# Five half tiles of the projection move from early slots to the last two

## The chip, the cores and the metric

The kernel runs on one core of one Trainium2 chip. Its engines are TensorE (PE; its weight loads are PEld), VectorE (DVE), ScalarE (ACT), GpSimd (POOL) and SyncE (SP, which issues the DMAs). Each engine works through its own instructions strictly in the written order and waits on semaphores for the others. The metric is the device time of one execution in microseconds, as a median of several runs; lower is better.

## The reference, cut to what matters

The input has 4 batches of 256 channels by 1024 tokens. It is normalised over the channels and over groups, turned into q, k and v by a convolution of 16 taps, and put through an attention of 4 heads; then a convolution of 5 taps projects the result, the residual is added, and a table step works on the normalised tokens.

```
qkv = conv1d_same(group_norm(xf, gn_gamma, gn_beta), qkv_w, qkv_b)
h = qkv_attention(qkv)
h = conv1d_same(h, proj_w, proj_b)
return (xf + h).reshape(b, c, *spatial)
...
x = x + _L0_conv_ref(_ln_c(x), ...)
t = _to_tokens(x)
t = t + _L0_ffn_ref(_ln_t(t))
```

The change touches the order in which the second convolution, the projection, is worked on beside the last piece of attention.

## The kernel before, in words

**Steps and slots.** Two pairs of heads times 4 batches make 8 steps of convolution. The attention of a step runs one step later, beside the next convolution. In the last step (the one that the change touches) there is no convolution left: the last attention runs beside the projection of the first three batches, and the projection of batch 3, which needs the result of that attention, follows. Each engine's program walks through slots 0 to 25. Slots 0 to 15 hold the 16 attention units, slots 16 and 17 the rest of the attention, slots 18 to 25 one projection tile of batch 3 each.

**An attention unit** is a score product on PE (L1372, into the PSUM tile psS or psT in turn), a maximum on DVE (L1713), a scaled copy and an exponential on ACT (L1104, L1111), a reciprocal on DVE (L1736), a scaled copy on ACT (L1121, the high half of the probabilities) and the low half on DVE (`prob_low`, L1690, issued one slot later). A DMA turns the result over, and PE multiplies it with the values (`second_product`, L1349 and L1353, one for two units, in the odd slots; the last two products, 6 and 7, both stand at the end of slot 17). Every second product but one completes a quarter of the heads, which is copied out by ACT (L951), summed on DVE (`heads_sum`, L1697), split by ACT (L960) and by DVE (`heads_low`, L1705). `second_product` 6 waits for the `heads_sum` of the quarter before it, because both use the PSUM tile psV.

**The projection** has 32 tiles, 8 for each batch. A tile is two halves of 15 matmuls (L1190): one half for each pair of heads; the second reads `staging`. Tile q is summed in one of three PSUM banks, cM, cP and cQ, in turn (`bank[q % 3]`). DVE then adds both parts to the residual (L1581, L1583) and takes statistics of the tile before (L1569); the second of these instructions gives the bank free. So the first half of tile q waits until DVE has emptied tile q - 3:

```
else:
    pe.wait_ge(S["pj_used"], q - 2)
```

After 8 tiles come the statistics, the norm (L254 to L1627, with a square root on ACT, L840) and the table step (L1643 to L1680) of that batch, in slots of their own. POOL adds the residual and the bias for each batch (`base`, L711 and L713, two long instructions) after ACT has scaled it (L931).

**The order.** In each slot DVE first takes its part of the attention (maximum, `prob_low` of the unit before, sums of heads, reciprocal), and after that the projection tiles whose second half lies in this slot on PE. PE takes the score product, then the halves of the slot, then the second product. A table, `halves`, says how many halves a slot holds; `beside` makes the slot of each half of the first three batches of it:

```
beside = [i for i in range(SLOTS) for _ in range(halves[i])]
for b in range(NB):
    for i in range(8):
        for p in range(PAIRS):
            late(beside[16 * b + 2 * i + p] if b < 3 else SLOTS + i, "tile", b, i, p)
```

The lists of ACT, POOL and SP for the last step do not depend on this table.

Of the kernel before, what the change touches and what calls it, by code (L numbers as in the profile page):

```python
# [42 lines left out]
UNITS = 16  # L43
SLOTS = 18
# [13 lines left out]
def build(nc, x_tok, w_qkv, b_qkv, gamma, beta, w_proj, b_proj, ident_in, group_in, ramp_in, out_tok):  # L58
    with ExitStack() as ctx:
# [261 lines left out]
                late(slot, "base", b, 2 * q)  # L321


        halves = [2 if i in (0, 4, 8, 12, 15, 16) else 3 for i in range(SLOTS)]
        assert sum(halves) == 3 * 16
        beside = [i for i in range(SLOTS) for _ in range(halves[i])]
        for b in range(NB):
# [1588 lines left out]
```

## Time and profile before

| what | value |
|---|---|
| median of 3 runs | 1009.72 us (1006.71 to 1011.4) |
| the profiled execution's own time | 1011.98 us |
| its span, first to last instruction | 1010.2 us |
| PE busy | 922.1 us (91%) |
| DVE busy | 736.9 us (73%) |
| ACT busy | 664.5 us (66%) |
| POOL busy | 348.2 us (34%) |
| mean granted TensorE clock | 0.978 |
| last step, first score product of its attention | 841.88 us |
| first projection matmul of batch 3 | 967.71 us |

The busy share is a mean over the whole kernel. The last step takes the last 168 us, and there PE, DVE, ACT and POOL wait for one another in turn; what a moved instruction is worth has to be read in that stretch, wait by wait. A matmul's duration in the rows overlaps with the next one's, so the time from start to start is the one to count with: 15 matmuls of a half begin 1.64 us after the 15 before them.

### The profile page before, as it was taken

The page shows a single profiled execution, that of the slowest core. Times are in us where ns is not written, and L with a number is a line of the kernel's source. Part 1 is how long each engine was busy: PE and PEld are TensorE (multiplying, and loading weights), DVE is VectorE, ACT ScalarE, POOL GpSimd, SP SyncE. Part 2 cuts the span into 40 slices and gives each one's busy share as a digit, 9 for nine tenths or more (in the row PEclk, how much of TensorE's full clock was granted, in tenths as well). Part 3 has the DMA queues.
Part 4 walks back from the last instruction along what each step waited for, and adds up shares of the span by engine and source line. Part 5 has one row for each costly group of instructions (what it writes and reads, how often), then busy time and mean ns, then how long its engine had stood idle before and what let it go on. Part 6 is the DMA issues. An engine that isn't in the chain of part 4 may idle for free.

```text
span 1010.2 us, 19614 instructions
## 1 busy us (share of the span) xinstructions
PE 922.1 (91%) x7826; PEld 739.4 (73%) x7826; DVE 736.9 (73%) x1234; ACT 664.5 (66%) x1112; POOL 348.2 (34%) x225
## 2 busy tenths in 40 slices
PE   2587889998999999999999999999999999898784
PEld 1476678786877787877788887887887868776663
DVE  6998958774777578897785656465646776879877
ACT  5758557783778378877886767465657585576531
POOL 2687934331550245365511211021102113313410
PEclk9989799999999999999999999999999999999987
DMA  8060235978798847576637544554656863362422
GB/s 297 1 220 23 84 139 117 217 176 205 166 223 191 197 105 157 129 209 133 127 85 189 137 84 111 154 104 91 130 137 153 183 174 73 97 137 68 107 62 84
DMA packets 291866, 138.32 MB, mean 137 GB/s; under 512 B 269120, under 2 KB 271552, under 8 KB 291264
## 3 DMA queue, kind: packets, MB, share of 16 engines
q1 hardware_dynamic: 291776, 137.08, 55.6%
q8 instruction: 62, 1.02, 0.4%
q14 instruction: 28, 0.23, 0.1%
HBM read 48.80 MB, written 16.95 MB: 65 GB/s over the span
## 4 chain that ended last, share of the span: by engine, by line
PE 56%; DVE 17%; ACT 9%; issue 5%; DMA 2%; POOL 2%; SPq 1%; ACTq 0%; POOLq 0%; DVEq 0%
PE cM L1235 13%; PE cQ L1235 12%; PE cP L1235 12%; PE psS L1372 4%; PE psV L1349 4%; PE psT L1372 4%; ACT arena L1111 3%; DVE smx L1713 3%; DVE arena L1690 3%; DVE W L1518 3%; PE psV L1353 3%; DMA arena<-arena 2%; PE cM L1190 1%; PE cP L1190 1%; DVE arena L1564 1%
## 5 line engine op out<-in xcount | busy, mean ns | idle before, releaser
L1235 PE MATMUL cM<-U,W 128*128 128x256 f16 x1728 | 206.0, 276 | 26.7 <-DVE U L1526 18.3
L1235 PEld LDWEIGHTS cM<-U,W 128*128 128x128 f16 x1728 | 170.2, 99 | 60.8 <-DVE U L1526 18.6
L1235 PE MATMUL cQ<-U,W 128*128 128x256 f16 x1728 | 204.5, 276 | 3.4 <-POOL U L647 3.4
L1235 PE MATMUL cP<-U,W 128*128 128x256 f16 x1728 | 202.3, 273 | 1.1 <-DVE W L1518 1.1
L1235 PEld LDWEIGHTS cQ<-U,W 128*128 128x128 f16 x1728 | 169.8, 98 | 34.8 <-POOL U L647 3.6
L1235 PEld LDWEIGHTS cP<-U,W 128*128 128x128 f16 x1728 | 168.0, 98 | 31.7 <-issue 1.4
L1690 DVE SCALAR_TENSOR_TENSOR arena<-arena,smx 128x1024 f16<-128x1024 f32 x128 | 177.2, 1384 | 12.1 <-ACT arena L1121 11.7
L726 POOL TENSOR_TENSOR ap<-ap 128x512 f32<-128x512 f32 x24 | 38.6, 1609 | 348.6 <-ACT ap L983 348.3
L1121 ACT ACTIVATE arena<-arena,smx 128x1024 f16<-128x1024 f32 x128 | 147.0, 1148 | 4.3
L1713 DVE TENSOR_REDUCE smx<-psS 128x1 f32<-128x1024 f32 x64 | 77.9, 1217 | 76.9 <-PE psS L1372 76.5
L1104 ACT ACTIVATE smx<-smx,tiny 128x1 f32<-128x1 f32 x128 | 37.3, 292 | 117.5 <-DVE smx L1713 116.9
L1713 DVE TENSOR_REDUCE smx<-psT 128x1 f32<-128x1024 f32 x64 | 78.0, 1218 | 29.0 <-PE psT L1372 28.7
L737 POOL TENSOR_TENSOR y_all<-y_all,ap 128x512 f32<-128x512 f32 x48 | 80.1, 1668 | 7.4 <-POOL y_all L737 4.1
L1111 ACT ACTIVATE arena<-psT,smx,tiny 128x1024 f32<-128x1024 f32 x64 | 77.1, 1205 | 2.1
L1111 ACT ACTIVATE arena<-psS,smx,tiny 128x1024 f32<-128x1024 f32 x64 | 77.1, 1205 | 2.1
L1349 PE MATMUL psV<-arena 128*128 128x256 f16 x512 | 68.0, 277 | 10.8 <-DMA arena<-arena 5.6
L690 POOL TENSOR_TENSOR wsum<-staging 128x512 f32<-128x512 f32 x24 | 45.4, 1905 | 61.6 <-DVE W L1518 56.0
L1372 PE MATMUL psT<-arena 128*128 128x512 f16 x256 | 65.7, 379 | 0.8 <-ACT arena L1111 0.8
L1372 PE MATMUL psS<-arena 128*128 128x512 f16 x256 | 66.2, 381 | 0.1
L1349 PEld LDWEIGHTS psV<-arena 128*128 128x128 f16 x512 | 50.3, 99 | 18.5 <-issue 12.1
L1736 DVE RECIPROCAL smx<-smx 128x1 f32<-128x1 f32 x128 | 20.4, 160 | 59.5 <-ACT arena L1111 59.1
L1117 ACT ACTIVATE smx<-smx 128x1 f32<-128x1 f32 x128 | 25.9, 202 | 39.8 <-DVE smx L1736 39.8
(220 smaller groups left out, 1324.5 us busy)
## 6 DMA issues: line engine op xcount, KB each, us to landing
U<-kept_u SPq DMA_DIRECT2D x21, 520.0 KB, 5.5
staging<-w_qkv SPq DMA_DIRECT2D x20, 512.0 KB, 5.4
wsum<-w_qkv SPq DMA_DIRECT2D x24, 256.0 KB, 4.2
U<-kept_u SPq DMA_DIRECT2D x7, 780.0 KB, 4.9
kept_u<-temp_b SPq DMA_DIRECT2D x9, 520.0 KB, 3.5
arena<-x_tok SPq DMA_DIRECT2D x8, 512.0 KB, 6.2
arena<-arena SPq DMA_DIRECT2D x16, 256.0 KB, 3.6
W<-x_tok SPq DMA_DIRECT2D x4, 1024.0 KB, 5.8
```

What stands on the lines that cost most here:

```text
L690: g.tensor_tensor(wsum[:, at % 2], pair[0], pair[1], ALU.add).then_inc(S["wsum_done"], 1)
L726: g.tensor_tensor(ap[:, 1:3, :], ap[:, 1:3, :], ap[:, 0:1, :].to_broadcast([P, 2, QUART]), ALU.add) \
L737: g.tensor_tensor(y[:, q * HALF:(q + 1) * HALF].rearrange("p (i r) -> p i r", r=2), y[:, HALF:T].rearrange("p (i r) -> p i r", r=2), ap[:, ...
L1104: a(smx[:, u % 2, 1:2], smx[:, u % 2, 0:1], ACT.Copy, scale=esc[:, m, 1:2]).then_inc(S["nb_done"], 1)
L1111: a(prob[:, u % 2, :], (psS, psT)[u % 2][:, :], ACT.Exp, bias=smx[:, u % 2, 1:2], scale=esc[:, m, 0:1], accum_out=smx[:, u % 2, 2:3]).then ...
L1121: a(phl[:, i % 3, 0, :], prob[:, i % 2, :], ACT.Copy, scale=smx[:, i % 2, 4:5]) \
L1235: last = mm(out, W[:, j, wl, c, QTAPS * (3 * family + third) + tap, :], u[:, ul, c, at + tap:at + tap + QUART], start=((g, c, t) in OPENER ...
L1349: mm(psV[:, at:at + QUART], vT[:, s, hd, :], probT[:, s, at:at + QUART], start=(s == 0), stop=False, skip_group_check=True)
L1353: last = mm(psV[R:R + D, at:at + QUART], vT[:, s, hd, D * hd:D * (hd + 1)], probT[:, 8 + s, at:at + QUART], start=False, stop=(s >= 6), sk ...
L1372: last = mm((psS, psT)[u % 2][:, h * HALF:(h + 1) * HALF], stack[:, hd, 0, u % 8 * P:(u % 8 + 1) * P], stack[:, hd, 1 + l, h * HALF:(h + 1 ...
L1690: v.scalar_tensor_tensor(phl[:, u % 3, 1, :], prob[:, u % 2, :], smx[:, u % 2, 4:5], phl[:, u % 3, 0, :], ALU.mult, ALU.subtract).then_inc ...
L1713: v.reduce_max(smx[:, i % 2, 0:1], (psS, psT)[i % 2][:, :], X).then_inc(S["mx_done"], 1)
```

## The change

One line, the table `halves`, is replaced.

```
-        halves = [2 if i in (0, 4, 8, 12, 15, 16) else 3 for i in range(SLOTS)]
+        halves = [3 if i in (1, 2, 4, 6, 9, 12) else 2 for i in range(UNITS)] + [5, 5]
```

UNITS is 16 and SLOTS is 18. Both tables sum to 48 halves, 16 for each of three batches:

```
slot     0  1  2  3  4  5  6  7  8  9 10 11 12 13 14 15 16 17
before   2  3  3  3  2  3  3  3  2  3  3  3  2  3  3  2  2  3
now      2  3  3  2  3  2  3  2  2  3  2  2  3  2  2  2  5  5
```

By the end of slot 15 there are 43 halves done before and 38 now, that is 21 whole tiles before and 19 now. A tile's work on DVE stands in the slot of its second half, so that moves too. ACT, POOL and SP keep their lists.

PE, from behind the score product of unit 15 (psT) to the last second product; psV rows are second products, cM, cP and cQ the banks of the tiles, `W` and `W,staging` the first and the second half of one. Before:

```order
L1372 MATMUL psT<-arena 128x512 x4
L1190 MATMUL cQ<-W,staging 128x256 x15
L1190 MATMUL cM<-W 128x256 x15
L1349 MATMUL psV<-arena 128x256 x8
L1353 MATMUL psV<-arena 64x256 x8
L1190 MATMUL cM<-W,staging 128x256 x15
L1190 MATMUL cP<-W 128x256 x15
L1190 MATMUL cP<-W,staging 128x256 x15
L1190 MATMUL cQ<-W 128x256 x15
L1190 MATMUL cQ<-W,staging 128x256 x15
L1349 MATMUL psV<-arena 128x256 x8
L1353 MATMUL psV<-arena 64x256 x8
```

Now, the same end of the list, from behind second product 5 (slot 15) on:

```order
L1190 MATMUL cP<-W 128x256 x15
L1190 MATMUL cP<-W,staging 128x256 x15
L1190 MATMUL cQ<-W 128x256 x15
L1190 MATMUL cQ<-W,staging 128x256 x15
L1190 MATMUL cM<-W 128x256 x15
L1190 MATMUL cM<-W,staging 128x256 x15
L1190 MATMUL cP<-W 128x256 x15
L1190 MATMUL cP<-W,staging 128x256 x15
L1190 MATMUL cQ<-W 128x256 x15
L1190 MATMUL cQ<-W,staging 128x256 x15
L1349 MATMUL psV<-arena 128x256 x8
L1353 MATMUL psV<-arena 64x256 x8
```

Five halves stand between second products 5 and 6 before, ten now: tiles 19 (cP), 20 (cQ), 21 (cM), 22 (cP) and 23 (cQ). Bank cP and bank cQ occur twice in this piece.

DVE, from `prob_low` of unit 15 (L1690, the first instruction of slot 16) to the first tile behind the last `heads_low` (slot 17). Before:

```order
L1690 SCALAR_TENSOR_TENSOR arena<-arena,smx 128x1024
L1697 SCALAR_TENSOR_TENSOR arena<-psV,arena 64x512
L1581 SCALAR_TENSOR_TENSOR W<-cM,tiny,W 128x256
L1583 SCALAR_TENSOR_TENSOR W<-cM,tiny,W 128x256
L1569 BN_STATS W<-W 128x6
L1705 TENSOR_TENSOR staging<-arena,staging 64x512
L1697 SCALAR_TENSOR_TENSOR arena<-psV,arena 64x512
L1705 TENSOR_TENSOR staging<-arena,staging 64x512
L1581 SCALAR_TENSOR_TENSOR W<-cP,tiny,W 128x256
```

Now:

```order
L1690 SCALAR_TENSOR_TENSOR arena<-arena,smx 128x1024
L1697 SCALAR_TENSOR_TENSOR arena<-psV,arena 64x512
L1581 SCALAR_TENSOR_TENSOR W<-cP,tiny,W 128x256
L1583 SCALAR_TENSOR_TENSOR W<-cP,tiny,W 128x256
L1569 BN_STATS W<-W 128x6
L1581 SCALAR_TENSOR_TENSOR W<-cQ,tiny,W 128x256
L1583 SCALAR_TENSOR_TENSOR W<-cQ,tiny,W 128x256
L1569 BN_STATS W<-W 128x6
L1705 TENSOR_TENSOR staging<-arena,staging 64x512
L1697 SCALAR_TENSOR_TENSOR arena<-psV,arena 64x512
L1705 TENSOR_TENSOR staging<-arena,staging 64x512
L1581 SCALAR_TENSOR_TENSOR W<-cM,tiny,W 128x256
```

Behind `prob_low` 15 and the `heads_sum` that second product 6 waits for, DVE emptied tile 21 before and empties tiles 19 and 20 now; tile 21 comes behind the last `heads_low` now, and tiles 22 and 23 follow it as before.

## Rows read from the trace of the kernel before

**Rows 1.** The page: the span, and busy time, share and instructions of two engines.

```profile
span 1010.2 us, 19614 instructions
...
PE 922.1 (91%) x7826; PEld 739.4 (73%) x7826; DVE 736.9 (73%) x1234; ACT 664.5 (66%) x1112; POOL 348.2 (34%) x225
```

**Rows 2.** Waits from 825 us on: who waited for whom, total, times, longest.

```profile
PE psV L1349 <- DVE arena L1697: 5.1, 1, 5.1
...
PE cP L1190 <- DVE W L1583: 3.7, 1, 3.7
...
PE cM L1190 <- DVE staging L1705: 2.8, 1, 2.8
```

**Rows 3.** PE timeline: start us, duration us, instruction, count, [idle before <- releaser].

```profile
917.92 3.21 PE L1190 MATMUL cP<-W 128*128 128x256 f16 x15 [3.69 <-DVE W L1583]
920.97 1.04 PE L1349 MATMUL psV<-arena 128*128 128x256 f16 x8
...
922.50 1.04 PE L1372 MATMUL psS<-arena 128*128 128x512 f16 x4
...
952.22 1.80 PE L1190 MATMUL cQ<-W,staging 128*128 128x256 f16 x15
959.13 1.86 PE L1349 MATMUL psV<-arena 128*128 128x256 f16 x8 [5.11 <-DVE arena L1697]
...
963.85 1.06 PE L1353 MATMUL psV<-arena 128*64 128x256 f16 x8
967.71 2.53 PE L1190 MATMUL cM<-W 128*128 128x256 f16 x15 [2.81 <-DVE staging L1705]
...
985.76 1.80 PE L1190 MATMUL cQ<-W 128*128 128x256 f16 x15
...
992.32 1.80 PE L1190 MATMUL cP<-W 128*128 128x256 f16 x15
```

**Rows 4.** DVE timeline of the last step, same columns.

```profile
889.79 0.20 DVE L261 RECIPROCAL nt<-nt 128x8 f32<-128x8 f32 x1 [0.84 <-ACT nt L840]
...
917.29 0.48 DVE L1583 SCALAR_TENSOR_TENSOR W<-cP,tiny,W 128x256 f32<-128x256 f32 x1
...
948.35 0.48 DVE L1583 SCALAR_TENSOR_TENSOR W<-cQ,tiny,W 128x256 f32<-128x256 f32 x1
...
951.75 0.20 DVE L261 RECIPROCAL nt<-nt 128x8 f32<-128x8 f32 x1 [0.28 <-ACT nt L840]
951.99 4.07 DVE L262 TENSOR_TENSOR nt<-nt 128x8 f32<-128x8 f32 x1
...
958.29 0.69 DVE L1697 SCALAR_TENSOR_TENSOR arena<-psV,arena 64x512 f32<-64x512 f32 x1
...
959.54 0.48 DVE L1583 SCALAR_TENSOR_TENSOR W<-cM,tiny,W 128x256 f32<-128x256 f32 x1
...
966.96 0.69 DVE L1705 TENSOR_TENSOR staging<-arena,staging 64x512 f16<-64x512 f32 x1 [0.69 <-ACT staging L960]
967.69 0.48 DVE L1581 SCALAR_TENSOR_TENSOR W<-cP,tiny,W 128x256 f32<-128x256 f32 x1
...
968.94 0.47 DVE L1581 SCALAR_TENSOR_TENSOR W<-cQ,tiny,W 128x256 f32<-128x256 f32 x1
...
995.79 0.48 DVE L1581 SCALAR_TENSOR_TENSOR W<-cP,tiny,W 128x256 f32<-128x256 f32 x1 [0.20 <-PE cP L1190]
```

**Rows 5.** ACT timeline of slot 8, and POOL's second instruction for batch 3.

```profile
899.38 0.28 ACT L1104 ACTIVATE smx<-smx,tiny 128x1 f32<-128x1 f32 x1
...
951.53 4.50 POOL L713 TENSOR_TENSOR W<-W 128x2048 f32<-128x2048 f32 x1
```

**Rows 6.** Busy time by stretch; behind POOL the granted TensorE clock, DMA share, GB/s.

```profile
918.00:919.00 1.00, 1.00 (x6) 0.68 (x6) 0.96 (x4) 1.00 (x3) 1.00 (x1) 0.50 1.18 271
...
921.00:922.00 1.00, 1.00 (x12) 0.72 (x11) 1.00 (x1) 1.00 (x2) 0.18 (x1) 1.00 0.00 0
...
964.00:965.00 1.00, 0.91 (x8) 0.38 (x6) 0.00 (x0) 0.05 (x1) 0.00 (x0) 0.50 0.00 0
```

## The prediction

> **What bounds the kernel now.** The page comes first: PE is busy for 91% of 1010.2 us and DVE for 73% [rows 1]. That is a mean, and the change lies in the last step alone, so I read the waits of that step next. There PE's longest wait is not for data of its own kind: a second product waits 5.1 us for the `heads_sum` on DVE (L1697), a projection tile waits 3.7 us for DVE to empty its bank (L1583), and the first tile of batch 3 waits 2.8 us for the last `heads_low` (L1705) [rows 2]. PE has little slack there, and where it has some, DVE is what it waits for.
>
> The timelines show how. PE ends its last half of batch 2 at 952.22 + 1.80 = 954.02 us and has nothing to do until second product 6 at 959.13; that one begins right behind `heads_sum` on DVE, which ends at 958.29 + 0.69 = 958.98 [rows 3, 4]. DVE in turn is late because of POOL: the small L262, issued at 951.99, ends at 956.06, and POOL's long L713 ends at 951.53 + 4.50 = 956.03 [rows 4, 5]. After second product 7 (last row 963.85 + 1.06 = 964.91) a chain over ACT and DVE ends with L1705 at 966.96 + 0.69 = 967.65; I call this point H. Batch 3 starts on PE at 967.71, and from there DVE is full to the end: its last tile waits only 0.20 us for PE [rows 3, 4].
>
> So the idle 5.1 us are there, and the change puts ten halves instead of five in front of them. The question is whether PE may run them there.
>
> **The change part by part: what PE may run.** A tile waits until DVE has emptied the tile three before, since there are three banks. The row for this is the wait of 3.69 us at 917.92: the L1583 that frees the bank ends at 917.29 + 0.48 = 917.77, and PE starts 0.15 later [rows 3, 4]. Before, tiles 22 and 23 needed tiles 19 and 20, which DVE emptied in slots 14 and 15. Now tiles 19 and 20 have their second halves in slot 16, so DVE empties them only behind `prob_low` 15 and `heads_sum`, that is behind the very point that PE is idle for. In PE's queue tile 22 stands in front of second products 6 and 7, which are held up behind it, and with them the chain to H and all of batch 3. The filler for the gap needs the end of the gap.
>
> **When the bank comes free.** In DVE's order tile 19 now has the place that tile 21 had, right behind `heads_sum`: its L1583 ends at 959.54 + 0.48 = 960.02 in the times of before [rows 4]. By slot 15 DVE has two tiles less to do. A tile costs it 1.25 us (967.69 to 968.94) [rows 4]; so the point moves forward by between 0 and 2.50 us. I take 0.56. The tile that leaves slot 5 lets ACT load its table for the first norm earlier; the square root then costs DVE the usual wait of 0.28 instead of 0.84 us [rows 4]. The other tile leaves slot 7, where it does not help, since in slot 8 ACT itself is behind: its L1104 at 899.38 has no idle time before it [rows 5]. In slots 10 and 11, and again in slot 15, DVE is held up by POOL, whose start hangs on ACT and moves by the same 0.56. Slot 12 gets a tile more and slot 13 one less; ACT's scaling in slot 12 now waits for tile 15, which DVE empties in the same slot, at a price of tenths that slot 13 gives back. Tile 19 is thus empty at 959.46, and PE starts tile 22 at 959.61.
>
> The Trainium skill ("SBUF — State Buffer", Who interferes with whom) says that a DVE instruction with two SBUF inputs is shut out for the whole of a GpSimd instruction that reads SBUF, and the other way round by who came first. The L262 row, ending 0.03 us behind L713, agrees. By it no relief of DVE gets past POOL's end, and only ACT can move that; without it 1.94 us more would, and the sum below would be smaller by that.
>
> **From tile 22 to H.** Four halves take 992.32 - 985.76 = 6.56 us, and a second product 922.50 - 920.97 = 1.53 us, two of them 3.06 [rows 3]. Together 9.62 us: 969.23 at the full clock.
>
> The clock is a term of its own. PE ends tile 21 early: it needs tile 18, whose place on DVE is the L1583 that ends at 948.35 + 0.48 = 948.83 [rows 4], less 0.56; with 0.15 and two halves of 1.64 PE is idle from 951.7 to 959.6, for 7.9 us. After the idle 3.69 us the granted clock was 0.50 (1.2 GHz) from the first matmul at 917.92 until about 920.9, and back at 1.00 (2.4 GHz) in the next microsecond [rows 3, 6]; after the idle 5.11 us it was 0.50 from 959.13 to the end of the second products at 964.91 [rows 3, 6]. At half the clock 3.0 us lose 1.5, and 5.8 us lose 2.9. I take 2.2, with these as near ends; no loss and a low clock through all 9.62 us are the far ones. Second product 7 ends at 971.43.
>
> The chain from there to H took 967.65 - 964.91 = 2.74 us and is not touched: H is 974.17 instead of 967.65, later by 6.52.
>
> **Behind H.** DVE has three tiles to empty there (21, 22, 23) instead of two: 1.25 us more in front of the table step and everything after it, of which the wait of 0.20 us before the last tile is won back: 1.05 [rows 4]. PE's first tile of batch 3 now waits for tile 21 to be emptied, about 1.0 us behind H plus 0.15; its 26.2 us (16 times 1.64) and 1.7 us for a low clock at the start, as before (from 967.71 to 992.32 + 2 times 1.64 = 995.6 is 27.9), end 29.1 us behind H. DVE reaches its last tile 995.79 - 967.65 + 1.05 = 29.2 us behind H. The two are level, so PE costs nothing beyond DVE's 1.05. If PE kept its clock DVE would still set the end.
>
> **The sum**: H is 6.52 us later (the 0.56 gained and the 2.2 lost are in it), and 1.05 follow behind it: 7.57 us. The profiled execution took 1011.98 us (span 1010.2, 1.8 around it), so it would take 1019.6. It lies 2.3 above the median of the runs, 1009.72, and the median of the changed kernel is put at **1017.3 us**. The ends of the own range: no shift and a loss of 2.9 give 7.57 + 0.56 + 0.7 = 8.8; the whole shift and no loss give 7.57 - 1.94 - 2.2 = 3.4.
>
> **The rivals.**
>
> *The gap is filled* (the other side). If tiles 22 and 23 did not have to wait, for instance because DVE got to tiles 19 and 20 while it waits for POOL, PE would work up to second product 6, which would begin at 958.98 - 0.56 + 0.15 = 958.6 at the full clock: 3.06 and 2.74 us later H is 964.4, 3.3 earlier; with 1.05 behind it the kernel is 2.2 us faster, 1007.5; with the whole shift 4.1, 1005.6. It decides at the point where the L1583 of tile 19 ends: before about 952, and this is what comes. For it speaks the idle 5.11 us; against it the order, in which tile 19 stands behind `prob_low` 15 and `heads_sum`. I give it 0.08. The Trainium skill ("TensorE: Matmul & The Clock Gate", Why this matters for your kernels) advises against idle gaps between bursts of matmuls, since the clock falls in them; that is the reason for such a filling, and by it alone the sum would be this rival's.
>
> *DVE's relief goes through*: two tiles less by slot 15 move everything 1.94 us more than I take, because the locks of POOL fall elsewhere, and the clock comes back soon. Then 7.57 - 1.94 = 5.6 us, down to 3.4: 1013.1 to 1015.3. For it speaks that DVE and not PE sets the pace of slots 7 to 15; against it ACT's row without idle time. 0.11.
>
> *The clock stays low* through all four halves and both second products: 9.62 us lost instead of 2.2, 1024.7. The longest low stretch with PE at work in this step was 5.8 us. 0.05.
>
> My forecast has 0.76.
>
> **How the numbers follow.** About 0.5% (5 us) is what a measurement of this kernel tells from no change. Slower by more, above 1014.8: the forecast but for 0.03 of it at the bottom of its own range, the low clock (0.05), and 0.02 of the relief: 0.80. Within: 0.03, 0.09 of the relief and 0.05 of the filled gap: 0.17. Faster: 0.03 of the filled gap. The range is 1012.5 to 1021: below it lie the filled gap and a little of the relief, above it the low clock, and the runs of before spread over 4.7 us themselves.
>
> **What would show it.** Right: behind unit 15's score product PE works through eight halves (tiles 18 to 21), then waits some 8 us in front of a cP tile, and an L1583 ends that wait; second product 6 follows the last half of tile 23 without a wait; DVE has three tiles in a row behind the last L1705, which comes some 6 us later than H did. Wrong: if that wait is short or ends before `heads_sum`, the mechanism is not there; if it ends at 957 instead of 959.6, the relief was larger; if H comes right but the end does not, the term behind H is wrong.

## The result and the profile after

The changed kernel takes 1019.0 us (median of 6 runs, 1015.92 to 1021.02), the kernel before 1010.75 us in 6 runs of the same chip: a ratio of 1.0084, with a 95% interval of 1.006 to 1.0109. It is slower by 8.3 us; 7.6 were forecast, and 1017.3 us as the median.

The profiled execution took 1021.0 us. Its page, span and busy time:

```profile
span 1019.2 us, 19614 instructions
...
PE 924.9 (91%) x7826; PEld 740.6 (73%) x7826; DVE 738.8 (72%) x1234; ACT 664.3 (65%) x1112; POOL 347.4 (34%) x225
```

The span is 9.0 us longer than in [rows 1], but not all of that is the change. The first score product of the last step starts at 843.22 us here and at 841.88 in the trace of before, and nothing moves ahead of it: 1.3 us are the difference of two executions. Below, times are therefore also counted from that first score product. From there to the end of the span it is 168.3 us before and 176.0 after: 7.7 us are the last step's.

PE's timeline after (start us, duration us, instruction, count, [idle before <- releaser]), the part that answers to [rows 3]:

```profile
929.57 1.63 PE L1349 MATMUL psV<-arena 128*128 128x256 f16 x8 [2.00 <-DVE arena L1697]
...
951.19 1.80 PE L1190 MATMUL cM<-W,staging 128*128 128x256 f16 x15
960.73 3.38 PE L1190 MATMUL cP<-W 128*128 128x256 f16 x15 [7.74 <-DVE W L1583]
963.91 1.84 PE L1190 MATMUL cP<-W,staging 128*128 128x256 f16 x15
...
968.86 1.04 PE L1349 MATMUL psV<-arena 128*128 128x256 f16 x8
...
971.37 0.63 PE L1353 MATMUL psV<-arena 128*64 128x256 f16 x8
975.92 3.36 PE L1190 MATMUL cM<-W 128*128 128x256 f16 x15 [3.92 <-DVE W L1583]
979.07 2.78 PE L1190 MATMUL cM<-W,staging 128*128 128x256 f16 x15
...
1002.97 1.80 PE L1190 MATMUL cP<-W,staging 128*128 128x256 f16 x15
```

After tile 21 PE stands still for 7.74 us in front of tile 22 (cP), and an L1583 of DVE ends that. Second product 6 follows the last half with no idle time, at 968.86 instead of 959.13. The wait of 5.1 us for `heads_sum` of [rows 2] is gone, because PE gets there long after it. The wait of 2.00 us at 929.57, for an earlier `heads_sum`, is new; e1 and e2 below have it too (2.0 us each) and are as fast as before.

DVE's timeline after, same columns, which answers to [rows 4]:

```profile
890.54 0.20 DVE L261 RECIPROCAL nt<-nt 128x8 f32<-128x8 f32 x1 [0.28 <-ACT nt L840]
...
949.00 0.48 DVE L1583 SCALAR_TENSOR_TENSOR W<-cM,tiny,W 128x256 f32<-128x256 f32 x1
...
952.65 4.06 DVE L262 TENSOR_TENSOR nt<-nt 128x8 f32<-128x8 f32 x1
...
958.94 0.69 DVE L1697 SCALAR_TENSOR_TENSOR arena<-psV,arena 64x512 f32<-64x512 f32 x1
...
960.19 0.48 DVE L1583 SCALAR_TENSOR_TENSOR W<-cP,tiny,W 128x256 f32<-128x256 f32 x1
...
974.05 0.69 DVE L1705 TENSOR_TENSOR staging<-arena,staging 64x512 f16<-64x512 f32 x1 [0.69 <-ACT staging L960]
974.77 0.48 DVE L1581 SCALAR_TENSOR_TENSOR W<-cM,tiny,W 128x256 f32<-128x256 f32 x1
975.29 0.48 DVE L1583 SCALAR_TENSOR_TENSOR W<-cM,tiny,W 128x256 f32<-128x256 f32 x1
...
1004.81 0.48 DVE L1581 SCALAR_TENSOR_TENSOR W<-cP,tiny,W 128x256 f32<-128x256 f32 x1 [0.91 <-PE cP L1190]
```

The L1583 of tile 19 ends at 960.67, right behind `heads_sum`, and PE starts 0.06 later. H, the end of the last `heads_low`, is 974.74: 131.5 us into the step instead of 125.8. Batch 3 waits for tile 21 to be emptied (L1583 at 975.29), 1.2 us behind H.

POOL's second instruction for batch 3 after, which answers to [rows 5], ends at 956.69, and L262 at 956.71:

```profile
952.19 4.50 POOL L713 TENSOR_TENSOR W<-W 128x2048 f32<-128x2048 f32 x1
```

The granted clock by stretch (the number behind POOL's busy time), which answers to [rows 6]: half (0.50) while the first half of tile 22 runs, full (1.00) from 964 on; half again when batch 3 begins, until about 981.

```profile
962.00:963.00 1.00, 1.00 (x6) 0.75 (x5) 0.94 (x2) 0.00 (x0) 0.00 (x0) 0.50 0.03 4
...
964.00:965.00 1.00, 1.00 (x11) 0.90 (x10) 0.00 (x0) 0.00 (x0) 0.00 (x0) 1.00 0.00 0
...
979.00:980.00 1.00, 1.00 (x7) 0.69 (x6) 0.91 (x3) 0.00 (x0) 0.00 (x0) 0.50 0.00 0
...
981.00:982.00 1.00, 1.00 (x10) 0.91 (x9) 0.86 (x8) 0.00 (x0) 0.00 (x0) 0.97 0.00 0
```

### The profile page after: what moved, and what is told of

It reads as the page before. It is cut to its first block, busy times and chain, and to the rows that moved or that the text cites. A ratio compares the mean times of both kernels' runs of the same rounds, so it can differ in the third digit from the quotient of the medians.

```text
span 1019.2 us, 19614 instructions
## 1 busy us (share of the span) xinstructions
PE 924.9 (91%) x7826; PEld 740.6 (73%) x7826; DVE 738.8 (72%) x1234; ACT 664.3 (65%) x1112; POOL 347.4 (34%) x225
## 4 chain that ended last, share of the span: by engine, by line
PE 59%; DVE 18%; ACT 8%; issue 4%; DMA 2%; SPq 1%; POOL 1%; ACTq 0%; DVEq 0%; POOLq 0%
PE cM L1235 14%; PE cQ L1235 12%; PE cP L1235 12%; PE psS L1372 4%; PE psV L1349 4%; PE psT L1372 4%; DVE W L1518 4%; DVE arena L1690 3%; ACT arena L1111 3%; PE psV L1353 3%; PE cP L1190 2%; DVE smx L1713 2%; PE cM L1190 2%; DMA arena<-arena 2%; PE cQ L1190 2%
## 5 line engine op out<-in xcount | busy, mean ns | idle before, releaser
L1235 PE MATMUL cM<-U,W 128*128 128x256 f16 x1728 | 208.5, 279 | 27.1 <-DVE U L1526 18.4
L1235 PE MATMUL cQ<-U,W 128*128 128x256 f16 x1728 | 201.7, 273 | 3.9 <-POOL U L647 2.1
L1235 PEld LDWEIGHTS cQ<-U,W 128*128 128x128 f16 x1728 | 168.6, 98 | 34.0 <-POOL U L647 2.4
L1690 DVE SCALAR_TENSOR_TENSOR arena<-arena,smx 128x1024 f16<-128x1024 f32 x128 | 178.7, 1396 | 11.7 <-ACT arena L1121 11.3
L1104 ACT ACTIVATE smx<-smx,tiny 128x1 f32<-128x1 f32 x128 | 37.3, 292 | 117.8 <-DVE smx L1713 117.1
```

Source lines behind the costliest of these rows:

```text
L1235: last = mm(out, W[:, j, wl, c, QTAPS * (3 * family + third) + tap, :], u[:, ul, c, at + tap:at + tap + QUART], start=((g, c, t) in OPENER ...
L1690: v.scalar_tensor_tensor(phl[:, u % 3, 1, :], prob[:, u % 2, :], smx[:, u % 2, 4:5], phl[:, u % 3, 0, :], ALU.mult, ALU.subtract).then_inc ...
```

## The experiments

The theory is the ring of three banks: tiles 22 and 23 may not start before DVE has emptied tiles 19 and 20, and that now lies behind `heads_sum`. Two rivals are that ten halves ahead of second product 6 are too much work, whoever waits, and that thinning the early slots upsets the attention. The table gives what each run measured; the five columns behind the time are from its trace, in us from the first score product of the last step, except that the last half's end (its start plus 1.64) is counted from H. Each kernel has one trace, of one execution, while the ratios come from 6 to 12 runs of it; the two need not agree to the last us.

| run | time, ratio to before (95% interval) | `heads_sum` ends | second product 6 starts | H | last half ends | span ends |
|---|---|---|---|---|---|---|
| before | 1 | 117.1 | 117.3 | 125.8 | H + 27.9 | 168.3 |
| after | 1.0084 (1.006 to 1.0109) | 116.4 | 125.6 | 131.5 | H + 29.9 | 176.0 |
| e1_psS | 0.9985 (0.9964 to 1.0006) | 116.4 | 116.6 | 123.9 | H + 30.0 | 168.5 |
| e2_drain | 1.0006 (0.9982 to 1.003) | 116.5 | 116.6 | 123.9 | H + 30.3 | 168.8 |
| e3_3and3 | 0.9988 (0.9967 to 1.0009) | 117.1 | 117.3 | 125.8 | H + 27.9 | 168.3 |
| e4_4and4 | 1.0041 (1.0021 to 1.0061) | 115.8 | 123.0 | 128.9 | H + 27.9 | 171.4 |
| e5_thin | 1.0007 (0.9985 to 1.0028) | 118.6 | 118.8 | 126.0 | H + 27.9 | 168.6 |
| e6_sp_first | 1.0026 (1.0011 to 1.0041) | 116.4 | 116.6 | 123.9 | H + 30.0 | 168.8 |
| e7_drain_all | 0.9988 (0.9975 to 1.0001) | 116.5 | 116.6 | 123.9 | H + 26.3 | 164.7 |
| e8_split_before | 0.9951 (0.9933 to 0.997) | 112.0 | 112.1 | 119.4 | H + 27.9 | 161.9 |
| e9_split_drain | 0.9952 (0.9936 to 0.9969) | 112.2 | 113.4 | 119.6 | H + 27.7 | 161.9 |
| e10_split_after | 1.0019 (1.0004 to 1.0034) | 111.5 | 120.7 | 126.6 | H + 29.9 | 171.1 |

**e1_psS: the wait taken away by other banks.**

```
+        def tile_bank(q):
+            return psS[:, (q - 22) * HALF:(q - 21) * HALF] if q in (22, 23) else bank[q % 3]
...
+                elif q in (22, 23):
+                    pe.wait_ge(S["e_done"], 16 * (STEPS - 1) + 15)
                 else:
                     pe.wait_ge(S["pj_used"], q - 2)
```

> The changed kernel, with tiles 22 and 23 summed in the two banks of the score tile psS, which is free once the exponential of unit 14 has read it; nothing else moves. Ring theory (PE is held up because tiles 22 and 23 need the banks of tiles 19 and 20, which DVE empties behind heads_sum): the wait of 7.7 us in front of tile 22 goes, PE runs the ten halves through, second product 6 starts within 0.3 us of the end of heads_sum at the full clock, and H (the last heads_low) comes about 9 us earlier than in the changed kernel; with three tiles still behind H the time is 1 to 4 us below the kernel before, so 8 to 12 below the changed one. Rival 'too much work' (ten halves ahead of second product 6 are too many, whoever waits): second product 6 still starts several us behind heads_sum and the time stays 5 to 8 us above before. Rival 'early slots' (thinning the early slots upsets the pace of the attention): early slots are as in the changed kernel, so 8 us above before.

PE's timeline of this run:

```profile
953.93 1.80 PE L1196 MATMUL psS<-W,staging 128*128 128x256 f16 x15
955.97 1.03 PE L1355 MATMUL psV<-arena 128*128 128x256 f16 x8 [0.24 <-DVE arena L1703]
...
958.92 1.03 PE L1355 MATMUL psV<-arena 128*128 128x256 f16 x8 [1.36 <-DMA arena<-arena]
...
964.44 3.36 PE L1196 MATMUL cM<-W 128*128 128x256 f16 x15 [3.92 <-DVE W L1589]
```

The wait is gone, with all ten halves still ahead of second product 6, and with it the slowdown. That refutes both rivals: the work and the early slots are those of the changed kernel. H is 7.7 us earlier than after, not 9: second product 7 now waits 1.36 us for the DMA of unit 15. And the 1.9 us won against before at H are lost behind it (H + 30.0 instead of 27.9). The runs lie 1.5 us below before, within the 1 to 4 expected, but the interval holds no change too.

**e2_drain: the wait taken away by DVE's order.** Of DVE's list alone, tiles 19 and 20 move from slot 16 to slot 15:

```
+        for i in (3, 4):
+            DVE_LATE[16].remove(("tile", 2, i, 1))
+            DVE_LATE[15].insert(at, ("tile", 2, i, 1))   # at: ahead of the norm
...
```

> The changed kernel, with DVE's work on tiles 19 and 20 moved from slot 16 to slot 15, ahead of the norm in which DVE waits for POOL anyway. Ring theory: tile 22 starts at about the end of tile 21 with no wait over 1 us, the 2.5 us of DVE work cost nothing because they lie inside the two stretches (2.2 and 3.9 us) in which L254 and L262 wait for POOL, and the time is that of the run with psS within 1.5 us: 1 to 4 us below before. If the norm's waits were not POOL's, heads_sum would come 2.5 us later and the time would be about that of before. Rivals 'too much work' and 'early slots': 5 to 8 us above before.

```profile
950.84 1.80 PE L1196 MATMUL cP<-W 128*128 128x256 f16 x15
```

This is tile 22: it has no wait in front of it, and `heads_sum` ends where it did after (116.5), with two tiles more in front of it: they cost DVE nothing, since it would have waited for POOL. The time is that of before and not 1 to 4 us below, for the same reasons as in e1.

**e3_3and3 and e4_4and4: how many halves may move.**

```
-        halves = [2 if i in (0, 4, 8, 12, 15, 16) else 3 for i in range(SLOTS)]
+        halves = [2 if i in (0, 4, 8, 12, 14, 15) else 3 for i in range(SLOTS)]                          # e3
+        halves = [2 if i in (0, 4, 8, 11, 12, 13, 14, 15) else 3 for i in range(UNITS)] + [4, 4]         # e4
```

> The table of before with one half moved from slot 14 to slot 16, so 3 and 3 in the last two slots: 42 halves, 21 whole tiles, are done by slot 15. Ring theory: tiles 19 and 20 are emptied by slot 15 as before, no tile waits for slot 16, and the time is that of before within 1.5 us. Rival in which each moved half costs its part: a fifth of 8 us, 1.6 above before (and then the idle time ahead of second product 6 would be shorter and H later); 'too much work' the same.

> The table of before with three halves moved from slots 11, 13 and 14 to the last two, 4 and 4 there: 40 halves, 20 whole tiles, are done by slot 15, and DVE empties tile 20 behind heads_sum in slot 16. Ring theory: only tile 23 waits (in bank cQ, for tile 20; tile 22 in cP does not), until the same point of DVE's list as in the changed kernel; two halves and the two second products follow, H is 3.3 us earlier than in the changed kernel and 2.5 later than before, two tiles stand behind H as before, and the time is 2 to 4 us above before. Rival in which each moved half costs its part: three fifths of 8 us, 5 above before, and no step between tiles 22 and 23.

e3 leaves 42 halves by slot 15, so tile 20 is still emptied there: every column is that of before. In e4 tile 20 is not:

```profile
950.57 1.81 PE L1190 MATMUL cP<-W 128*128 128x256 f16 x15 [0.68 <-DVE W L1583]
...
961.74 3.38 PE L1190 MATMUL cQ<-W 128*128 128x256 f16 x15 [7.72 <-DVE W L1583]
```

Tile 22 in cP runs and tile 23 in cQ waits, as the ring has it. H is 3.1 us later than before and 2.6 earlier than after. The time is 4.1 us above before by the ratio and 3.1 by the trace; alone it would not tell the ring from a cost for each half, but that cost foresees neither e3 (1.6 us above before for the one half, outside the interval) nor the bank at which PE stops.

**e5_thin: the early slots alone.**

```
+        halves = [3 if i in (1, 2, 4, 6, 9, 12) else 2 for i in range(13)] + [4, 4, 3, 2, 3]
```

> The early slots 0 to 12 are thinned as in the change, but the halves go to slots 13 to 15 (4, 4 and 3), and the last two slots keep 2 and 3 as before; 43 halves are done by slot 15. Rival 'early slots': as slow as the changed kernel, 6 to 8 us above before. Ring theory: no wait of a tile for slot 16; the time is that of before within 2 us, a little later at most since DVE gets its tiles in slots 13 to 15 in front of the norm (up to 2.5 us if they are not hidden by POOL's stretch).

As fast as before: thinning the early slots is not the cause.

**e6_sp_first: the wait kept, the queue behind it emptied.** In PE's list second products 6 and 7 move ahead of tile 22:

```
+                                if i == 17 and (e, *tile) == (2, 6, 0):
+                                    second_product(k, 6)
+                                    second_product(k, 7)
                                 project(e, *tile)
...
```

> The changed kernel, with second products 6 and 7 moved in PE's list ahead of tiles 22 and 23; DVE's list and the banks are as in the changed kernel, so tile 22 still waits for tile 19. Ring theory with PE's order as its second half (the harm comes from what is queued behind the waiting tile): second product 6 starts right behind heads_sum, H comes 6 to 8 us earlier than in the changed kernel, tiles 22 and 23 run in the time in which ACT and DVE finish the heads, batch 3 starts some 2 us later than before, counted from the start of the last step; time 0 to 2 us above before, 6 to 8 below the changed kernel. Rival 'early slots' or 'third tile behind H' as the main cause: still 5 us or more above before.

```profile
954.42 1.86 PE L1349 MATMUL psV<-arena 128*128 128x256 f16 x8 [6.79 <-DVE arena L1698]
...
958.94 1.81 PE L1190 MATMUL cP<-W 128*128 128x256 f16 x15
...
965.50 1.80 PE L1190 MATMUL cM<-W 128*128 128x256 f16 x15
```

Banks and DVE's order are those of the changed kernel, yet H is as early as in e1. So the harm is not that tile 22 waits but what stands behind it. Tiles 22 and 23 then push batch 3 to 3.7 us behind H; without idle time ahead of it it keeps the full clock. The time is 2.6 us above before (0.5 by the trace) and 5.8 below after by the two ratios: a little outside the 0 to 2 above and 6 to 8 below that were expected.

**e7_drain_all: the term behind H.** e2, and the tiles 21 to 23 of DVE's slot 17 move to the end of slot 16.

> The run e2_drain with DVE's work on tiles 21, 22 and 23 moved from behind the last heads_low to slot 16, behind heads_sum and ahead of the other heads_low, where DVE had 4 to 10 us of idle time. It measures the term behind H: with three tiles there, batch 3 began 1.2 us behind H, PE was idle for 3.9 us and its first halves ran at the low clock. Now batch 3 should begin within 0.2 us of H, after 2.8 us of idle time, with a shorter low stretch; counted from the first score product of the last step to the end of the span, 166.5 to 168 us instead of 168.75 (before 168.3). If the three tiles behind H cost nothing on PE's side, 168.75 stays.

```profile
963.25 1.81 PE L1199 MATMUL cM<-W 128*128 128x256 f16 x15 [2.80 <-DVE staging L1714]
964.89 1.80 PE L1199 MATMUL cM<-W,staging 128*128 128x256 f16 x15
```

Batch 3 starts right behind H, and here the clock did not fall: the two halves start 1.64 us apart, and the last half ends at H + 26.3. That is 4.0 us less than in e2 in the traces, more than expected: 1.1 for the earlier start and 2.9 for the clock. The runs give less, 1.8 us below e2 by the two ratios and 1.2 below before, with an interval that just holds no change; the profiled execution, at 1005.83 us, lies 1.7 below the median of its runs. Whether the clock stayed full in the others is not shown.

**e8, e9 and e10: POOL's instructions in eight pieces.**

```
-                    g.tensor_tensor(base[:, k % 2], base[:, k % 2], xf[:, k % 2], ALU.add).then_inc(S["c_z"], 1)
+                    for t in range(8):
+                        g.tensor_tensor(base[:, k % 2, t], base[:, k % 2, t], xf[:, k % 2, t], ALU.add).then_inc(S["c_z"], 1)
...
```

The second instruction is cut in the same way, and the counts that others wait for are multiplied by eight. e8 has the table of before, e9 is e7 with this, e10 the changed kernel with this.

> The kernel before, with each of POOL's two long instructions for a batch (L711, L713; 128x2048) cut into eight of 128x256, one for each tile. If DVE's small instructions wait for the end of POOL's instruction (L262 took 4.07 us and ended with L713), no DVE instruction of the last step is drawn out by more than 0.8 us any more; L254, L262, L1690 and L1564 get back 2.2, 3.9, 3.4, 2.7 and 1.8 us, heads_sum comes 3 to 6 us earlier, the idle time of PE ahead of second product 6 shrinks below 2 us, and the time falls by 3 to 6 us. If DVE is shut out as long as POOL has any work in its list, or POOL is slowed by as much, the time stays within 1.5 us of before.

> POOL's instructions cut into eight as in e8_split_before, on top of e7_drain_all (the changed table, DVE's work on tiles 19 and 20 ahead of the norm and on 21 to 23 behind heads_sum). If what e7 gained over before (the end of the low clock in front of batch 3 and of the tiles behind H) and what e8 gained (no long waits of DVE for POOL) are separate, the two add: from the first score product of the last step to the end of the span 159 to 161 us (before 168.3, e7 164.7, e8 161.9), 1 to 3 us below e8 and 5 to 9 below before. If with the shorter POOL pieces PE is the bound up to second product 6, the five moved halves are on its path whoever empties the banks, and the time is that of e8 within 1 us or above it.

> The changed kernel with POOL's instructions cut into eight, nothing else. The claim is that the gate for tile 22 (the L1583 of tile 19 behind heads_sum) hangs on the end of POOL's work for batch 3: then the gate comes 4 to 6 us earlier, the wait in front of tile 22 shrinks from 7.7 to 2 to 4 us, and the time falls by 5 to 7 us against the changed kernel, to 1 to 3 us above before; it stays 5 to 8 us above e8_split_before, since the ring wait and the third tile behind H are still there. If the gate hung on DVE's own work, the wait and the time would stay as in the changed kernel within 2 us.

The timelines of e8, DVE's, POOL's and PE's (L712 and L715 are the L711 and L713 of before):

```profile
942.96 0.65 DVE L254 TENSOR_SCALAR nt<-ln 128x8 f32<-128x8 f32 x1
...
945.01 0.63 DVE L262 TENSOR_TENSOR nt<-nt 128x8 f32<-128x8 f32 x1
```

```profile
940.24 6.06 POOL L712 TENSOR_TENSOR W<-W 128x256 f32<-128x256 f32 x8 [21.89 <-ACT W L932]
946.38 6.50 POOL L715 TENSOR_TENSOR W<-W 128x256 f32<-128x256 f32 x8
```

```profile
951.12 1.03 PE L1350 MATMUL psV<-arena 128*128 128x256 f16 x8 [0.39 <-DVE arena L1698]
```

L262 is held up for 0.63 instead of 4.07 us though POOL works on: DVE is shut out for one instruction of POOL, not for its whole list. `heads_sum` ends 5.1 us earlier, PE's idle time ahead of second product 6 is 0.39 us instead of 5.11, and the kernel is 4.9 us faster than before (6.4 by the traces): with e9 the fastest of all runs, and ahead of both kernels.

PE's timeline of e9:

```profile
952.22 1.80 PE L1200 MATMUL cQ<-W,staging 128*128 128x256 f16 x15
953.86 1.04 PE L1359 MATMUL psV<-arena 128*128 128x256 f16 x8
...
960.11 3.22 PE L1200 MATMUL cM<-W 128*128 128x256 f16 x15 [2.80 <-DVE staging L1715]
963.17 1.80 PE L1200 MATMUL cM<-W,staging 128*128 128x256 f16 x15
```

e9 is no faster than e8, so the two gains don't add, as the second branch of its expectation has it. PE is the bound up to second product 6: that one follows the tenth half with no idle time, 1.3 us behind `heads_sum`, and H is 0.3 us later than in e8. Behind H the clock fell here, after the same 2.80 us of idle time as in e7: the first half of batch 3 takes 3.06 us from start to start instead of 1.64, and the last half ends at H + 27.7.

In e10, the changed kernel, `heads_sum` too comes 4.9 us earlier and the time falls by 6.5 us by the two ratios: the gate of tile 22 did hang on POOL. But the wait shrinks only to 5.49 us, where 2 to 4 were expected, since PE gets to tile 22 earlier as well:

```profile
951.37 3.38 PE L1191 MATMUL cP<-W 128*128 128x256 f16 x15 [5.49 <-DVE W L1584]
```

It stays 6.8 us above e8 by the two ratios and 9.2 by the traces; with POOL's long instructions the change costs 8.4 by the ratio and 7.7 by the traces. So cutting them does not take away the cost of the ring; whether it changes its size is not told by these numbers.

## Why the prediction was right, point by point

- **What PE may run.** Right, and shown: the wait of 7.74 us stands in front of the cP tile, ended by the L1583 of tile 19. Two other ways to free the banks (e1, e2) take it away, e3 and e4 place it at the tile that the ring names, and e6 shows that the price lies in the second products queued behind.
- **When the bank comes free.** Forecast 0.56 us earlier than before, measured 0.69 (`heads_sum`, 116.4 instead of 117.1 us into the step). The step it was to come from is there: DVE's wait at 890.54 is 0.28 us instead of 0.84. That DVE gets no further than POOL lets it is borne out by L262 in this trace, ending 0.02 us behind L713, and by e8 and e10, where the gate moves by 5 us once POOL's instructions are short. But POOL's own start can move with DVE's relief. In e4, with one tile less by slot 15 and the halves taken from slots 11, 13 and 14, POOL's L711 starts 103.2 us into the step instead of 104.5, and `heads_sum` ends 1.3 earlier, the whole 1.25 of a tile; in the changed kernel L711 starts at 103.8. So how much goes through hangs on which slots are thinned. The rival in which all of it goes through here, 2.5 us, did not come.
- **From tile 22 to H.** Forecast 9.62 us of work and 2.2 for the clock, measured 960.73 to 972.00, 11.27 us: 1.65 for the clock, low from 960.73 to 964. H is 5.75 us later (in the step), 6.52 were forecast. The clock rival, low all through, did not come.
- **Behind H.** The term that was mis-sized: 1.05 forecast, 1.9 measured (span end at H + 44.5 instead of 42.6). I had PE and DVE level and DVE setting the end. DVE's share was right: without its wait it would reach its last tile 29.2 us behind H, as forecast. But PE sets the end: its first tile starts 1.18 us behind H, as forecast, but after 3.92 us of idle time it lost 2.5 us to the clock (975.92 to 981.68 for two halves, 3.28 at the full clock) instead of 1.7, and DVE's last tile waits 0.91 for it instead of 0.20. In the traces with two tiles behind H the last half ends at H + 27.9, with three at H + 29.9 to 30.3; that difference was worth as much as the filling of the gap. With none it ends at H + 26.3 in e7 and at H + 27.7 in e9, so a part of it is the clock, which the number of tiles alone does not set.
- **The filled gap**, priced at 2.2 us below before, is what e1 and e2 built. At H it is right in kind (1.9 us earlier), but behind H all of it is lost, and the time is that of before. The price left out the wait for the DMA of unit 15 (1.3 us) and the clock behind H.
- Both misses, 0.8 too much before H and 0.9 too little behind it, cancel, and that is luck: the total came closer than its parts. With 1.3 us of another execution the profiled span grew by 9.0 us.

What stays open: why the first score product starts between 837.9 and 844.8 us in these traces, and why the clock fell at the start of batch 3, with 2.80 or 2.81 us of idle time ahead of it, in before, e3, e4, e5, e8 and e9 and not, with 2.80, in e7.

## What to carry to other kernels

Filler for a gap must be able to run in that gap: with a ring of n buffers, the item n places back has to be emptied ahead of the event that ends the gap, and otherwise the filler blocks everything queued behind it. Look at the consumer's list, not only at the idle engine's. And ask first what makes the gap: here it was made by long GpSimd instructions, and cutting these in pieces (4.9 us below before in e8) was worth more than any order of the tiles that was tried.

## What the runs showed of the hardware that was not expected

GpSimd's two instructions of 128x2048 for batch 3, 5.08 and 4.50 us in the trace of before, take 6.06 and 6.50 us when each is cut in eight, so 3.0 us more of GpSimd together. This still gives back more than it costs: DVE's small L262 gets in between two pieces after 0.63 us. Nearly the same idle time of PE (2.80 and 2.81 us) was followed by the full clock in one trace (e7) and by half in six others (before, e3, e4, e5, e8 and e9).
